# Attention with LayerNorm and a LoRA feed-forward on one core: query chunks of 512 instead of 256, with the PSUM banks, the p tiles and the order of work laid out anew

## The reference

```python
xn = layernorm(x)                                   # over the 256 features
q, k, v = xn @ wq.T + bq, xn @ wk.T + bk, xn @ wv.T + bv
attn = softmax(einsum('bqd,bkd->bqk', q, k) * 256 ** -0.5)
lilora = up_aux @ (lora_up @ (lora_down @ down_aux))
ffn = xn @ W.T + b + xn @ lilora.T
out = x + attn @ v + ffn
```

## Time and profile before

| | us |
|---|---|
| median of 3 runs | 530.42 |
| lowest and highest run | 530.37, 530.45 |
| the profiled execution, own time | 530.57 |
| its span, first to last instruction | 528.8 |
| PE busy | 516.6 (98%) |
| PE weight loads busy | 487.2 (92%) |
| DVE busy | 433.1 (82%) |
| POOL busy | 337.6 (64%) |
| ACT busy | 286.1 (54%) |

### The profile page before, as it was taken

One profiled execution on the slowest core, in us unless ns is written; L12 is line 12 of the kernel. 1 busy time (PEld: TensorE's weight loads), 2 busy tenths in 40 slices (PEclk: granted clock), 3 DMA queues, 4 the chain that ended last, 5 costly groups with the idle time before them and its releaser, 6 DMA issues.

```text
span 528.8 us, 10083 instructions
## 1 busy us (share of the span) xinstructions
PE 516.6 (98%) x3716; PEld 487.2 (92%) x3716; DVE 433.1 (82%) x1162; ACT 286.1 (54%) x747; POOL 337.6 (64%) x206
## 2 busy tenths in 40 slices
PE   4999999999999999999999999999999999999996
PEld 4689999999999999999999999999999999999996
DVE  4788889888897888878989789887889778777896
ACT  2746757346575466555762575734666546344442
POOL 2837653898548965789549895489755895433330
DMA  8020321003300032001130031100300000000001
GB/s 245 26 81 1 100 64 37 22 21 102 99 21 21 2 100 100 22 21 45 56 102 21 20 101 52 50 20 22 100 21 20 21 17 6 22 20 21 21 6 56
DMA packets 10721, 25.17 MB, mean 48 GB/s; under 512 B 2075, under 2 KB 3761, under 8 KB 9777
## 3 DMA queue, kind: packets, MB, share of 16 engines
q1 hardware_dynamic: 9344, 24.38, 14.0%
q10 hardware_dynamic: 1328, 0.16, 0.2%
HBM read 16.15 MB, written 8.39 MB: 46 GB/s over the span
## 4 chain that ended last, share of the span: by engine, by line
PE 94%; DVE 4%; DMA 1%; issue 1%; ACT 0%; ACTq 0%; DVEq 0%
PE s_ps L908 12%; PE s_ps L910 12%; PE s_ps L909 12%; PE o_ps L995 11%; PE o_ps L993 11%; PE o_ps L991 11%; PE g_ps L908 8%; PE g_ps L910 8%; PE g_ps L909 8%; DMA bk_col<-in_L_attn_bk 1%; DVE s L776 1%; DVE tile_max L742 1%; DVE p_lo L788 1%; PE g_ps L927 0%; PE s_ps L1005 0%
## 5 line engine op out<-in xcount | busy, mean ns | idle before, releaser
L466 POOL TENSOR_TENSOR p_lo<-s,p_hi 128x1024 fp32r<-128x1024 f32 x62 | 149.5, 2412 | 159.1 <-ACT p_hi L593 138.4
L585 ACT ACTIVATE s<-s,e 128x256 f32<-128x256 f32 x256 | 109.4, 498 | 125.8 <-DVE s L776 125.7
L991 PE MATMUL o_ps<-v_hi,p_hi 128*128 128x258 f32 x512 | 144.8, 283 | 1.3 <-DVE p_lo L788 1.0
L995 PE MATMUL o_ps<-v_hi,p_lo 128*128 128x258 f32 x512 | 144.7, 283 | 0.0
L993 PE MATMUL o_ps<-v_lo,p_hi 128*128 128x256 f32 x512 | 144.3, 282 | 0.0
L908 PE MATMUL s_ps<-xt_hi,zt_hi 128*128 128x256 f32 x504 | 142.5, 283 | 0.0
L910 PE MATMUL s_ps<-xt_hi,zt_lo 128*128 128x256 f32 x504 | 142.4, 283 | 0.0
L909 PE MATMUL s_ps<-xt_lo,zt_hi 128*128 128x256 f32 x504 | 142.3, 282 | 0.0
L742 DVE SCALAR_TENSOR_TENSOR tile_max<-s_ps,e,tile_max 128x256 f32<-128x256 f32 x221 | 106.8, 483 | 21.9 <-PE s_ps L910 12.2
L991 PEld LDWEIGHTS o_ps<-v_hi,p_hi 128*128 128x128 f32 x512 | 96.7, 189 | 4.0 <-DVE p_lo L788 1.4
L908 PEld LDWEIGHTS s_ps<-xt_hi,zt_hi 128*128 128x128 f32 x504 | 96.3, 191 | 2.5 <-issue 0.3
(11 more groups left out here) (127 smaller groups left out, 753.0 us busy)
## 6 DMA issues: line engine op xcount, KB each, us to landing
out<-base SPq DMA_DIRECT2D x31, 256.0 KB, 2.5
x_sb<-in_L_attn_x SPq DMA_DIRECT2D x7, 1024.0 KB, 5.9
x_t<-in_x_t SPq DMA_DIRECT2D x6, 1024.0 KB, 6.0
x_sb<-in_L_attn_x SPq DMA_DIRECT2D x4, 256.0 KB, 6.3
s<-in_L_attn_wk SPq DMA_DIRECT2D x1, 256.0 KB, 3.0
s<-in_L_attn_wq SPq DMA_DIRECT2D x1, 256.0 KB, 6.0
s<-in_L_attn_wv SPq DMA_DIRECT2D x1, 256.0 KB, 7.3
s<-in_L_ffn_W SPq DMA_DIRECT2D x1, 256.0 KB, 7.6
```

The lines of the kernel that those rows point to most:

```text
L466: nc.gpsimd.tensor_tensor(p_lo[g % 2][:, keys, :], s[:, keys, :], p_hi[g % 2][:, keys, :].bitcast(f32), ALU.subtract)\
L585: nc.scalar.activation(s[:, n, :], s[:, n, :], ACT.Exp, bias=e[b % 2][:, n:n + 1])\
L991: nc.tensor.matmul(o_ps[u][:, 0:D + ONES], p_hi[g % 2][:, n, q], v_hi[i][:, n, :], start=(n == 0), stop=False)
L995: mm = nc.tensor.matmul(o_ps[u][:, 0:D + ONES], p_lo[g % 2][:, n, q], v_hi[i][:, n, :], start=False, stop=(n == TILES - 1))
```

## The change

A chunk becomes 512 queries (`Q = BANK`): two chunks to a batch, 16 in all, and a turn has eight score tiles that fill a bank each, and four query tiles of products.

- **PSUM.** Eight banks of scores are wanted, and two of the eight banks are `o_ps`. Key tiles 0 to 3 lie in `s_ps`, tiles 4 and 5 in the two banks of the groups, and tiles 6 and 7 again in `s_ps` 0 and 1. For that ACT copies tiles 0 and 1 out to `raw` in SBUF (`make_raw`) once their maximum is taken. DVE shifts the six that are held (`HELD`), in the order 4, 5, 6, 7, 2, 3, and POOL the two copied ones (`shift_raw`).
- **Waits that come with it.** Score tiles 0 to 3 wait for the third to sixth shift of the chunk before, tiles 4 and 5 for all groups begun so far to be split out, tiles 6 and 7 for `raw`. A group at places 1 to 3 waits for the shift of its bank.
- **Kept once.** `p_hi` and `p_lo`, `zt_hi` and `zt_lo` are single; `p_hi` of a chunk waits until all products of the chunk before are made. `top` lies in `tile_max`. In the last chunk p goes to buffers that are free by then (`p_pair`). p is handled in pairs of tiles, 1024 elements to an instruction.
- **Order.** Groups stand after score tile 1 and after query tiles 1, 2 and 3. With two turns to a batch, the work on the next batches moves: statistics between the tile maxima of the first turn, `stat_cols` and `stat_rows` ahead of the softmax of the second; `xt_hi` and `xt_lo` at its end; `p_hi(g)` beside the scores of g+1.

The diff, cut to its core:

```diff
-    Q = BANK // 2
+    Q = BANK
-    KEYS = BANK // Q
-    SB = TILES // KEYS
+    RAW = 2
+    HELD = TILES - RAW
+    ORDER = (4, 5, 6, 7, 2, 3, 0, 1)
...
+        def score_bank(n):
+            return (s_ps + g_ps + s_ps[0:RAW])[n]
...
-        LATER = [{2: 4, 3: 5}, {0: 6, 2: 7, 3: 8}, {0: 9, 2: 10, 3: 11}, {0: 12, 1: 13, 2: 14, 3: 15}]
+        FIRST = [{0: (0, 1), 1: (2, 3), 2: (4, 5), 3: (6, 7)}, {0: (8,), 1: (9, 10), 2: (11, 12), 3: (13, 14, 15)}]
+        LATER = [{1: (4, 5), 2: (6, 7), 3: (8, 9)}, {0: (10,), 1: (11, 12), 2: (13, 14), 3: (15,)}]
...
+            def shift_raw(g):
+                pool.wait_ge(raw_made, RAW * (g + 1))
+                pool.wait_ge(top_made, g + 1)
+                wait(pool, p_lo_made, PAIRS * g)
+                nc.gpsimd.tensor_tensor(s[:, 0:RAW, :], raw[:, :, :],
+                                        top[:, :].unsqueeze(1).to_broadcast([PT, RAW, Q]), ALU.subtract)\
+                  .then_inc(raw_shifted, 1)
...
+            def make_raw(g, n):
+                act.wait_ge(tile_max_made, TILES * g + n + 1)
+                wait(act, raw_shifted, g)
+                nc.scalar.activation(raw[:, n, :], score_bank(n)[:, :], ACT.Copy).then_inc(raw_made, 1)
...
                 if j == 0:
-                    wait(act, pv_mm, QT * (g - 1))
+                    wait(act, pv_mm, QT * g if g < LAST else TILES * (B - 1))
+                nc.scalar.activation(p_pair(g, p_hi_sb, j), s_pair(j), ACT.Copy).then_inc(p_hi_made, 1)
...
+            for g in range(LAST):
+                b, c = divmod(g, CHUNKS)
+                for n in range(TILES):
+                    scores(g + 1, n)
+                    if n == 1:
+                        groups_of_next(b, c, 0)
+                for u in range(QT):
+                    p_times_v(g, u)
+                    if u > 0:
+                        groups_of_next(b, c, u)
```

More of the change, by code:

```diff
@@ L902, in _ @@
+                make_groups_lo(b, c, 2)
+            for t in range(TILES - QT - 1, TILES):
                 make_out(B - 1, t)
@@ L911, in split_products, with group @@
                 return mm
-            def group(b, k):
+            def group(b, k, shifts=0):
                 ps = group_bank(b, k)
@@ L947, in group, with groups_of_next, scores @@
                 mm.then_inc(group_mm, 1)
-            def group_of_next(b, c, place):
-                if group_at(b, c, place) is not None:
-                    group(b + 1, group_at(b, c, place))
-            def scores(g, j):
+            def groups_of_next(b, c, place):
+                for k in groups_at(b, c, place):
+                    group(b + 1, k, HELD * (CHUNKS * b + c + 1) + 1 if place else 0)
+            def scores(g, n):
                 b, c = divmod(g, CHUNKS)
@@ L975, in p_times_v @@
-            def p_times_v(g, tiles, beside=None):
+                if c == 0 and n in (0, TILES // 2):
+                    pe.wait_ge(group_done, groups(b, NT + DT - 1 if n == 0 else 2 * NT - 1))
+                if n < RAW:
+                    wait(pe, shifted, HELD * (g - 1) + 3 + n if g else 0)
+                elif n < 4:
+                    wait(pe, shifted, HELD * (g - 1) + 3 + n if g else 0)
+                    if g == 0:
+                        pe.wait_ge(group_done, NT + n + 1)
+                elif n < 6:
+                    pe.wait_ge(group_done, groups_begun(g - 1) if g else 2 * NT)
+                else:
+                    pe.wait_ge(raw_made, RAW * g + n - 5)
+                    pe.wait_ge(tile_max_made, TILES * g + n - 5)
@@ new lines, in p_times_v @@
+                wait(pe, out_made, TILES * b + t - 1)
+                q = slice(u * PT, (u + 1) * PT)
+                o = o_ps[u % 2]
+                for j in range(PAIRS):
+                    if u == 0 and g == LAST:
+                        pe.wait_ge(last_p_lo_made, j + 1)
+                    elif u == 0:
+                        pe.wait_ge(p_lo_made, PAIRS * g + j + 1)
+                    for m in range(2):
+                        n = ORDER[2 * j + m]
+                        first, last = (j, m) == (0, 0), (j, m) == (PAIRS - 1, 1)
+                        hi, lo = p_pair(g, p_hi_sb, j)[:, m, q], p_pair(g, p_lo_sb, j)[:, m, q]
+                        nc.tensor.matmul(o[:, 0:D + ONES], hi, v_hi[i][:, n, :], start=first, stop=False)
+                        nc.tensor.matmul(o[:, 0:D], hi, v_lo[i][:, n, :], start=False, stop=False)
+                        mm = nc.tensor.matmul(o[:, 0:D + ONES], lo, v_hi[i][:, n, :], start=False, stop=last)
@@ L1048, in _ @@
             mm.then_inc(delta_mm, 1)
-            for j in range(1, SB):
-                scores(0, j)
+            for n in range(1, 4):
+                scores(0, n)
             pe.wait_ge(wv_lo_made, 1)
```

481 lines of the change are left out of this document (234 added, 247 removed).

## The result

The changed kernel takes **586.51 us** (median of 4 runs, 586.02 to 587.05) against 530.39 (4 runs, 530.24 to 530.45) before: ratio 1.106, 95% interval 1.104 to 1.108. The predicted 572.0 was 14.5 us too low; the sign was right, and the range of 549 to 588 holds the time near its upper end. The profiled execution is 586.13 us, its span 584.3.

What follows compares the result with a forecast made beforehand. TensorE (PE), busy 98% of the span, was taken as the bound. 530.6 - 3.9 - 2.4 + 18.3 + 15.9 + 10.2 + 0.45 + 3.3 = 572.4, less 0.15: 572 us, range 549 to 588.

Steps and rivals of the forecast that it cites:

- PE's saving: Score matmuls: 1536 of 256 columns (183.1 us) become 768 of 512 (179.2 us), 3.9 us less, bounds 3 and 5.
- The 2.4 of gaps at the end of before: Last chunk of the old kernel: PE waits for DVE about 2.4 us in four gaps, which go after the change.
- Second turns: c = 1, b = 0 to 5: stat_cols and its transposes delay tile maxima, top and shifts; 3.05 us x 6 = 18.3.
- The 0.2 before the first output: Second turns: after waiting 2.85 us for a shift, PE waits 0.2 more for the first output.
- First turns: c = 0, b = 1 to 6: PE waits in query tile 0 for POOL's fourth p_lo; 2.65 us x 6 = 15.9.
- the backlog of statistics: First turns: batch b+2's statistics on DVE, hidden by the p_lo wait, would alone cost 1.7 us.
- e_sum hidden with 0.9 of cover: ACT's e_sum waits for prod and delays the exponentials; costs nothing, with 0.9 us cover, beyond which each microsecond counts six times.
- Start and first turn: Batch 0's groups 14 and 15 2.7, next scores 0.65, score tile 4 3.1, shift 0 1.15, third query tile 2.6; sum 10.2.
- Turn 14: No groups there: the third query tile comes at S+5.7 (S: scores end) and waits for the output at S+9.0; 3.3 us.
- Turn 13: Taken as a clean turn, losing 0.45 us.
- A clean turn: With no other DVE work, the first shifted bank and first output come after PE wants them; at least 0.45 us lost.
- the rival about the clock: Gaps of 3 us bring PE's lower clock back, costing 1.5 us at each of some 14 gaps: 592 us; chance 0.07.

Runs made afterwards that it cites:

- e3: Changed kernel with ACT's 16 stat_cols copies moved from behind the four p_hi of second turns to ahead of the third: 567.63 us.
- e5: e4 with ACT's e_sum of batches 2 to 7 moved from ahead of the exponentials to behind the fourth: 575.17 us.
- e4: Changed kernel with POOL's two xt_lo of a batch moved from ahead of the chunk's four p_lo to behind them: 599.59 us.
- e6: Changed kernel with the edits of e3 and e5 together: 555.75 us.
- e1: Changed kernel with the second query tile's 24 matmuls issued twice in six second turns, filling PE's gap with 17.2 us more work: 578.71 us.
- e2: e1 with only 12 of the second query tile's matmuls issued twice, to halve the gap: 580.15 us.
- e7: e6 with the first output behind the second shift (in turn 14 ahead of all) and the second half of the statistics behind the shifts: 547.07 us.
- e8: Changed kernel with DVE's stat_rows transposes back behind the shifts and POOL's shift_raw ahead of both norm_x_t: 578.50 us.
- e9: e7 with e8's moves, e3's copies back in place, turn 0's transposes' split ahead of p_hi, turn 14's second output ahead of the fifth shift: 548.91 us.

## Why the prediction was right, and where it failed

**Bound and direction: right.** PE lost its full occupation, and the two repeated chains did it.

**PE's saving, 3.9: too small.** The prediction gave score matmuls of 512 columns the spacing of a group, 0.233. In the changed kernel they are closer than groups. Its own order of time, six scores' spacings and then six of a group:

```profile
39.99 0.39 PE L958 MATMUL s_ps<-xt_hi,zt_lo 128*128 128x512 f32 x1
...
41.35 0.39 PE L958 MATMUL s_ps<-xt_hi,zt_lo 128*128 128x512 f32 x1
41.58 0.40 PE L956 MATMUL o_ps<-vf_hi,xt_hi 128*128 128x512 f32 x1
...
42.97 0.40 PE L956 MATMUL o_ps<-vf_hi,xt_hi 128*128 128x512 f32 x1
```

That is 0.227 for a score and 0.232 for a group. Over the whole trace the scores at full rate stand 0.2276 apart in the mean, and those of 256 columns before stood 0.1195 apart, so the saving is 183.5 - 174.8 = 8.7 us, well outside the bounds of 3 and 5. Why scores go faster than groups of the same size, no run shows. In the books the rest is lower by 6.8 (4.4 to 6.0 in the experiments): 8.7 less for the scores and 0.65 less for the first score, at 23.80 instead of 24.45, against some 2.5 of small steps that the two columns don't count. The 2.4 of gaps at the end of before, which the sum takes off, are 1.6 in the books (2.1 with the shorter ones), and they did go.

**Second turns, 18.3:** measured 20.7: 3.15 to 3.53 before the group, 19.3 in all, and 0.33 at the group's second matmul in four of six. The 0.2 before the first output did not come. e3 shows the cause by moving only the copies: the 19.3 fall to 6.6.

**First turns, 15.9:** measured 16.0, at the fourth `p_lo` 15.8 us into the turn, as computed. One detail was off: the third `p_lo` already makes PE wait, so the loss is two gaps. e5 confirms the cause: with `xt_lo` behind `p_lo` no wait on `p_lo` is left, and the gaps go from 2.66 to 1.10 in five first turns. That 1.10 is the backlog of statistics that the prediction put at 1.7 if it stood alone.

**e_sum hidden with 0.9 of cover:** right in the changed kernel, where no wait of that kind is seen; e4 exceeds the cover and pays 2.57 five times and 3.46 once.

**Start and first turn, 10.2:** measured 8.7: 2.50 for 2.7 before group 14, 2.55 for 3.1 before score tile 4, 0.89 for 1.15, 2.47 and 0.26 for 2.6 around the third query tile. The 0.65 for the next scores did not come. Turn 14: 3.23 for 3.3. Turn 13: 0.3 for 0.45. All stalls together: 48.9 against 48.2. A clean turn, which the prediction put at a loss of 0.45, costs 1.04 and more when it has copies and transposes in it at all (e6).

**The step that failed** is the price of a gap. The forecast took it as costing its own length; the rival about the clock was held at 0.07 and left out of the sum. After the gaps of the six second turns, two of the start's, turn 14's and two of the first turns' pairs, PE ran at half rate for 2 to 6 us, which adds 1.0 to 2.5 each, 15.3 in all; the rival's 1.5 for each of 14 gaps comes to 21, against 11 stretches at 1.4. The row that stood against it, gaps of up to 0.7 us at the end of before that did nothing, says nothing on gaps of 3 us; and the row for it, 0.21 us at 12 us, is the spacing of 256 columns in every half-rate stretch. e1 shows that the gap is the cause: with the gap filled, the clock stays. Against the sum's 572.4, the profiled 586.1 has 15.0 more of half rate, 1.5 more of gaps and 2.9 less in the rest, where the sum had only the 3.9; so the two sizes that were off worked against each other, and that was luck.

The Trainium skill (TensorE: Matmul & The Clock Gate, "HAM oscillation — how this bites in real kernels") describes a kernel that falls between the levels because PE waits for transfers, and advises to restructure so that it does not. Here the waits are for DVE and POOL, and the effect is the same: 0.427 us a matmul of 512 columns, which agrees with the figure of 426.7 ns that the page gives at the lower level ("Wait — 56ns, not 53.3ns?"). At the upper one the same section gives 215.7 ns. The rows here show 227.6 for scores and 232 for groups, and these are what counts for this kernel.

**The range:** 549 to 588 held 586.5 only since it had been stretched to the clock's case; the forecast's own range ended at 586.

Open: why of six identical pairs of gaps in first turns two (after, e1) or three (e2, e3) have a half-rate stretch behind them, and the others none. By the rows, what PE did just before is the same in all. And whether any order of this staging reaches 530: it wants both the early transposes, for POOL, and late ones, for the shift, and the versions here trade one against the other. e7's 21.3 us of gaps against the 4 to 7 by which the rest is lower leave no room without shortening DVE's chain or POOL's passes.

## What to carry to other kernels

When chunks grow and buffers become single, compute the dependent chain once (here: last score, maximum, top, first shift, output) against the work that covers it, with everything that stands in those engines' orders beside it; the 8.7 us saved on the scores of the whole kernel were lost again, in gaps alone, within two of its batches. Take a matmul's spacing from rows of the same product where there are any: the one for scores was 2% off, and that made the saving 5 us too small. Where a PE that was full gets gaps of about 3 us, price each at its length plus, as here, 1.0 to 2.5 us for what runs at half rate behind it, and look for shorter gaps rather than fewer: in these traces isolated gaps of 1.0 to 2.1 us had no such cost. Before moving a step out of a late chain, write down who waits for it next: three of the moves here (e4, e8, e9) gave most or all of their gain back to the next engine in line.

## What the runs showed of the hardware that I had not expected

- PE's clock falls inside a kernel whose PE is busy for 91%: after a gap of 3.15 us the group starts at 0.23 to 0.30 spacing and is at 0.42 less than 1 us later (the rows at 252.49; in four of the six second turns it is there from the second matmul on); the granted clock reads 0.61 over the 4 us with it and 1.00 over the gap itself.
- How often half rate followed within 2 us of a gap, in the ten traces of changed kernels, for gaps with no other of 0.9 us or more within 4 us: 1.0 to 2.1 us, none of 32; 2.5 to 2.9 us, 16 of 26; 3.1 to 3.8 us, 31 of 33. The length alone does not decide: the two exceptions are the 3.46 of e4 and a 3.14 in the start of e5.
- 1.17 and 1.49 with six matmuls between were followed by half rate in two of six places (after, e1) and in three of six (e2, e3), though none of 25 single gaps of 1.0 to 1.5 us was.
- Matmuls of 512 columns for scores stand 0.2276 us apart at full rate, those for groups 0.232, in the same trace.
- The same program, run again, was granted a mean clock of 0.993 or of 1.000 (e7), with 2.7 us between the times. The kernel before varied by 1.0 us in the seven runs beside e1 (529.81 to 530.81), e9 by 6.2 in four.
